# Mixed adapter values in the idle rows of the third down tile, and the next body's gate products ahead of the end of this one

## Chip, cores and metric

One NeuronCore of one Trainium2 chip runs the whole kernel. The metric is the device time of one launch, in microseconds (us), as the median of three runs. In what follows PE is the matrix engine (TensorE), DVE is VectorE, ACT is ScalarE, POOL is GpSimd and SP is SyncE, which only issues transfers here.

## What is computed

A gated state-space layer is followed by a mixture of experts; both are added to `x` (4 batches of 512 tokens, width 512). The change lies in the mixture's down projections. Cut to that, with E = 64 mask slots in 8 groups (experts) of 8 adapters of rank 8, I = 352 hidden values:

```
def _fused_linear(x, W, qa, qb, scale, w):
    out = x @ W.T
    a = einsum('th,krh->tkr', x, qa)
    b = einsum('tkr,khr->tkh', a, qb)
    mix = einsum('tkh,tk->th', b, w)
    return out + scale[None, :] * mix
def expert(...):
    xe = x + w @ muW.T
    gate = silu(_fused_linear(xe, gW, gqa, gqb, gs, w))
    up = _fused_linear(xe, uW, uqa, uqb, us, w)
    return _fused_linear(gate * up, dW, dqa, dqb, ds, w)
```

For the down projection of one expert, `x` above is `gate * up` (512 tokens by 352 values), `a` times `w` are 8 x 8 = 64 mixed adapter values for each token, and `qb` takes those 64 to the 512 outputs. A sum over the 8 experts, weighted per token, and the two halves of a shared expert are added to the layer's input.

## The kernel before

Every float is split into a high part (rounded to the type that PE takes here) and a low part (the rest), and a product is three matmuls: high by high, high by low, low by high. All matmuls have 512 columns at most. There are four batches (b = 0 to 3); each has ten bodies, `s = 10 b` to `10 b + 9`: two for the halves of the shared expert and eight for the experts, e = 0 to 7 (**routed** bodies). Beside the routed bodies of batch b, ACT, DVE and POOL work through the state-space scan of batch b + 1 (64 tiles, ten in most bodies), so batch 3 has none. The 64 tiles of batch 0 come ahead of the first body, and in batch 0 the weights of bodies 3 to 9 are also split on the way (ACT `hi`, DVE and POOL `lo_piece`) and stored to scratch memory; later batches load them from there. The engines' order is written out by hand, one function per engine and body, and semaphores tie them together.

What PE does in a routed body (`routed` in the tensor block):

- `up(s, m, 0)` and `up(s, m, 1)` for the three tiles of hidden values (128, 128 and 96 of them): 12 matmuls each, gate products into bank `bg[m]` (b_g0, b_g1, b_g0), up products into `bu[m]` (b_u0, b_u1, b_u0), and 8 half-height adapter matmuls after each pair. `up_waits(s, 0)` waits for the weights `gm0`, for DVE to be done with the third hidden tile of the body before, and for `dve_dawf` of the body before, since that was read from b_g0. `up(s, 0, 1)` waits for the first add of the body before, which frees b_u0.
- `qa`, `qa_mask`: 13 matmuls for the next body's adapters, into b_q.
- `down(s, tc, ms)`: for one of four groups of 128 tokens (tc) and some of the three hidden tiles (ms) three matmuls per tile: 9 in all for one bank. The third hidden tile fills 96 of the 128 rows. The banks by tc are b_g1, b_u1, b_q, b_u0.
- `adapter_a`: nine matmuls into b_g0, after which `pe_a` tells DVE.
- `adapter_b(s, tc)`: two matmuls into the same bank as `down(s, tc)`: `daw_s` by the high and by the low part of `qb`. `pe_dn` is raised after the second. The four groups go in the order 3, 0, 1, 2 (`DONE`).

Between `adapter_a` and `adapter_b` three steps run on other engines: `daw_first` (DVE: mixed adapter values `dawf` from b_g0), `daw_round` (ACT: high part `rnd`), `daw_low` (DVE: `daw_s`, whose rows 0 to 63 hold the high part and rows 64 to 127 the low part; `dawf` holds its 64 values twice). `add_down` (DVE) then adds each finished bank to `xx`, in the order of `DONE`. In bodies with scan tiles DVE has further work between these: a tile's scan between `daw_first` and `daw_low` (slot e), the low part of `qb` and another tile after `daw_low` (slot f), then the adds, then two tiles (slot a) and the first `hidden` of the next body, which waits for ACT's tanh and with it for `pe_gu`, raised by PE after `up(s, 0, 1)` and its adapters.

In e = 7 the scan is over; in batches 0 to 2 PE there transposes the next batch's normalised input in two steps (`xn_transposed`), one before and one after `down(s, 2)`.

SP issues all weight transfers in program order. In the bodies of batch 0 from 3 on `raw_store` writes each finished tile to scratch (`dwt`, down weights, in one transfer, `dqt`, the adapters' down weights `qa` and `qb`, in one); the store of a tile stands ahead of the next load into the raw buffer that it came from.

Of the kernel before, what the change touches and what calls it, by code (L numbers as in the profile page):

```python
# [26 lines left out]
P = 128  # L27
# [10 lines left out]
IC = 3  # L38
# [18 lines left out]
def gated_ssm_moe(nc, x, ctxT, gu, dd, pre, rr, cst, inv, out):  # L57
    with ExitStack() as ctx:
# [13 lines left out]
        Q_D = IC * P + H  # L72
# [176 lines left out]

        pe_lgT, act_lgT, pe_lg, dve_rt, act_ex, pe_wdT, act_wdT, pe_fl = (  # L250
# [48 lines left out]
        def scaled(kind, s):  # L299
            return 2 * (s - 3) + (1 if kind == "qb" else 2)  # L300

# [45 lines left out]
        def _(sp):  # L347
# [47 lines left out]
            def store(kind, s):  # L395
                sp.dma_start(scr[kind][w_index(s)], tile_of[kind][:].bitcast(F32).rearrange("p a n -> p (a n)")
                             ).then_inc(dma_st[kind], 16)
# [9 lines left out]
            def load(kind, s):  # L407
                free(sp, kind, s)
                sp.wait_ge(dma_st[kind], 16 * stored_before(kind, s))
                sp.dma_start(tile_of[kind][:].bitcast(F32).rearrange("p a n -> p (a n)"), scr[kind][w_index(s)]  # L410
                             ).then_inc(dma_t[kind], 16)
# [179 lines left out]
        def _(pe):  # L591
# [212 lines left out]
            def down(s, tc, ms=range(IC)):  # L804
# [14 lines left out]
                for m in ms:  # L819
                    if tc == 0:  # L820
                        pe.wait_ge(dve_hl, IC * s + m + 1)
                    n = 3 * m
                    k = slice(0, IW[m])
                    o = m * H
                    for v, hl_ in ((hh, 0), (hl, 0), (hh, 1)):
                        i = mm(down_bank(s, tc)[:], v[k, m, t], dwt[k, hl_, o:o + H], start=(n == 0),  # L826
                               stop=(n == 8 and not is_routed(s)))
                        n += 1
                return i

# [131 lines left out]
        def _(act):  # L962
# [6 lines left out]
            def hi(kind, s):  # L969
                k = piece[kind, s]  # L970
                act.wait_ge(dma_raw[slot_of[k]], 16 * use_of[k])
                if kind in ("dq", "qb"):
                    act.wait_ge(pool_scale, scaled(kind, s))
                free(act, kind, s)
                need(act, dma_st[kind], 16 * stored_before(kind, s))
                rounded(tile_of[kind][:, 0], raw[slot_of[k]][:, 0:width[kind]]).then_inc(act_hi[slot_of[k]], 1)

            def hi_0(n):
# [4 lines left out]
                if n >= 4 and (kind[0] == "g" or kind == "dw"):  # L983
                    act.wait_ge(dma_st[kind], 16 if s == 2 else 32)
# [36 lines left out]
            def round_ctx(nb):  # L1021
                act.wait_ge(dma_ctx, 16 * (nb + 1))
                if nb > 0:
                    need(act, pe_dn, LC * NX * (nb - 1))
                    for k in ("dq", "qb"):
                        act.wait_ge(dma_st[k], 16 if nb == 1 else 16 * NF)
# [435 lines left out]
        def _(dve):  # L1462
# [481 lines left out]
```

## Time and profile before

| what | value |
|---|---|
| runs | 1695.51 us (median of 3), 1692.44 to 1696.01 |
| profiled execution: span from first to last instruction | 1685.8 us |
| PE busy | 1568.4 us (93%), 6856 matmuls |
| DVE busy | 1155.5 us (69%) |
| POOL busy | 737.8 us (44%) |
| ACT busy | 617.2 us (37%) |
| chain of work that ended last | PE 63%, DVE 18%, issue 5%, ACT 5%, POOL 4%, DMA 3% |

The profile comes from one execution, whose span is the second row. Its time from outside isn't listed; the median of the runs is 9.7 us above the span, which is what lies before the first and after the last instruction, together with the difference between executions. PE's busy time counts each matmul from its start to a modelled end, and neighbours overlap; how close matmuls follow each other is read from the starts in the timeline.

### The profile page before, as it was taken

The page shows a single profiled execution, that of the slowest core. Times are in us where ns is not written, and L with a number is a line of the kernel's source. Part 1 is how long each engine was busy: PE and PEld are TensorE (multiplying, and loading weights), DVE is VectorE, ACT ScalarE, POOL GpSimd, SP SyncE. Part 2 cuts the span into 40 slices and gives each one's busy share as a digit, 9 for nine tenths or more (in the row PEclk, how much of TensorE's full clock was granted, in tenths as well). Part 3 has the DMA queues.
Part 4 walks back from the last instruction along what each step waited for, and adds up shares of the span by engine and source line. Part 5 has one row for each costly group of instructions (what it writes and reads, how often), then busy time and mean ns, then how long its engine had stood idle before and what let it go on. Part 6 is the DMA issues. An engine that isn't in the chain of part 4 may idle for free.

```text
span 1685.8 us, 19547 instructions
## 1 busy us (share of the span) xinstructions
PE 1568.4 (93%) x6856; PEld 1155.1 (69%) x6856; DVE 1155.5 (69%) x1634; ACT 617.2 (37%) x971; POOL 737.8 (44%) x537
## 2 busy tenths in 40 slices
PE   3787799798888999999999999999999999999999
PEld 2343377566666677777777777777777777777776
DVE  5798964788999867487888755778888553333333
ACT  5545443444454434443343244333433321111111
POOL 4488510489898801077777301376786000000000
PEclk8799999899999999999999999999999999999999
DMA  7688627688787664765667445587665456566552
GB/s 251 215 285 315 254 80 253 201 290 297 270 289 286 253 255 172 248 228 205 232 238 258 152 161 196 202 275 257 238 208 180 175 200 210 184 222 222 195 181 85
DMA packets 111473, 375.87 MB, mean 223 GB/s; under 512 B 20176, under 2 KB 45776, under 8 KB 94864
## 3 DMA queue, kind: packets, MB, share of 16 engines
q1 hardware_dynamic: 101904, 340.81, 57.8%
q10 hardware_dynamic: 9472, 33.82, 5.8%
q8 instruction: 55, 0.90, 0.2%
q14 instruction: 42, 0.34, 0.1%
HBM read 304.33 MB, written 70.25 MB: 222 GB/s over the span
## 4 chain that ended last, share of the span: by engine, by line
PE 63%; DVE 18%; issue 5%; ACT 5%; POOL 4%; DMA 3%; SPq 0%; ACTq 0%; DVEq 0%; POOLq 0%
PE b_g L735 14%; PE b_u L735 14%; PE b_u L826 7%; DVE ring L1493 4%; PE b_g L826 3%; PE b_q L781 3%; PE b_q L826 3%; PE b_g L799 2%; DVE ring L1499 2%; PE b_g L766 2%; DVE tt L1467 2%; POOL ring L1392 2%; PE b_g L759 1%; POOL yx L1401 1%; DVE z L1467 1%
## 5 line engine op out<-in xcount | busy, mean ns | idle before, releaser
L1392 POOL TENSOR_TENSOR ring<-du,rep 128x512 f32<-128x512 f32 x256 | 344.5, 1349 | 151.4 <-DVE du L1571 91.9
L735 PE MATMUL b_g<-xnb,gm 128*128 128x512 f32 (+1 forms) x1440 | 356.2, 396 | 0.9 <-DVE xnb L1470 0.9
L735 PE MATMUL b_u<-xnb,gm 128*128 128x512 f32 (+1 forms) x1440 | 349.1, 391 | 0.0
L1493 DVE TENSOR_TENSOR_SCAN ring<-b_a,ring 128x512 f32<-128x512 f32 x256 | 310.8, 1214 | 15.7 <-ACT b_a L964 8.4
L1401 POOL TENSOR_TENSOR yx<-yx,ring 128x512 f32<-128x512 f32 x192 | 261.8, 1364 | 130.4 <-DVE ring L1499 129.9
L735 PEld LDWEIGHTS b_g<-xnb,gm 128*128 128x128 f32 (+1 forms) x1440 | 252.1, 179 | 89.1 <-issue 24.6
L735 PEld LDWEIGHTS b_u<-xnb,gm 128*128 128x128 f32 (+1 forms) x1440 | 257.1, 179 | 71.1
L1467 DVE SCALAR_TENSOR_TENSOR tt<-tt,b_g 128x512 f32<-128x512 f32 (+1 forms) x120 | 82.1, 684 | 222.7 <-ACT tt L964 222.5
L964 ACT ACTIVATE b_a<-delta,a_neg 128x512 f32<-128x512 f32 x256 | 173.6, 681 | 113.9 <-DVE ring L1493 113.9
L964 ACT ACTIVATE tt<-b_g 128x512 f32<-128x512 f32 (+1 forms) x120 | 71.1, 593 | 316.7 <-PE b_u L766 286.3
L826 PE MATMUL b_u<-dwt,hhl 128*128 128x512 f32 (+1 forms) x720 | 185.4, 394 | 0.0
L826 PEld LDWEIGHTS b_u<-dwt,hhl 128*128 128x128 f32 (+1 forms) x720 | 135.7, 189 | 30.0 <-issue 0.5
L1470 DVE TENSOR_TENSOR hhl<-tt,hhl 128x512 fp32r<-128x512 f32 (+1 forms) x120 | 89.9, 749 | 84.4 <-ACT hhl L964 84.4
L964 ACT ACTIVATE hhl<-tt 128x512 fp32r<-128x512 f32 (+1 forms) x120 | 75.4, 628 | 177.8 <-DVE tt L1467 177.8
L1499 DVE TENSOR_TENSOR ring<-ring,b_d 128x512 f32<-128x512 f32 x192 | 126.7, 660 | 0.0
L826 PE MATMUL b_g<-dwt,hhl 128*128 128x512 f32 (+1 forms) x360 | 100.1, 401 | 12.7 <-issue 7.4
L781 PE MATMUL b_q<-xnb,qat 128*128 128x512 f32 x384 | 97.7, 404 | 4.7 <-DVE qat L1470 4.7
L799 PE MATMUL b_g<-hhl,dqt 128*128 128x512 f32 (+1 forms) x288 | 77.5, 409 | 25.5 <-DVE tt L1467 13.6
L781 PEld LDWEIGHTS b_q<-xnb,qat 128*128 128x128 f32 x384 | 71.0, 191 | 30.0 <-issue 8.9
L826 PEld LDWEIGHTS b_g<-dwt,hhl 128*128 128x128 f32 (+1 forms) x360 | 67.1, 191 | 32.7 <-issue 10.0
L1467 DVE SCALAR_TENSOR_TENSOR tt<-tt,b_u 128x512 f32<-128x512 f32 (+1 forms) x120 | 82.2, 685 | 4.1
L799 PEld LDWEIGHTS b_g<-hhl,dqt 128*128 128x128 f32 (+1 forms) x288 | 53.8, 194 | 45.0 <-issue 17.6
(254 smaller groups left out, 2120.2 us busy)
## 6 DMA issues: line engine op xcount, KB each, us to landing
gm<-scr_gm SPq DMA_DIRECT2D x64, 1024.0 KB, 6.8
dwt<-scr_dw SPq DMA_DIRECT2D x32, 1536.0 KB, 6.8
rep<-bc_d ACTq DMA_DIRECT2D x64, 512.0 KB, 5.8
gm<-scr_gm SPq DMA_DIRECT2D x32, 768.0 KB, 4.4
dqt<-scr_dq SPq DMA_DIRECT2D x25, 896.0 KB, 9.1
scr_gm<-gm SPq DMA_DIRECT2D x20, 1024.0 KB, 7.5
scr_dw<-dwt SPq DMA_DIRECT2D x10, 1536.0 KB, 6.2
qat<-scr_qa SPq DMA_DIRECT2D x25, 512.0 KB, 10.2
```

The source lines that it names most:

```text
L735: i = mm(out_b[0:IW[m], :], w, v, start=(n == 0), stop=(n == 11 and not is_routed(s)))
L766: i = mm(out_b[0:IW[m], :], qbt[rows, hl_, cols], v[rows, :], start=False, stop=(k == 2))
L781: mm(b_q[:], w, v, start=(n == 0), stop=False)
L799: i = mm(b_g0[:], w, v, start=(n == 0), stop=(n == 8))
L826: i = mm(down_bank(s, tc)[:], v[k, m, t], dwt[k, hl_, o:o + H], start=(n == 0), stop=(n == 8 and not is_routed(s)))
L964: return nc.scalar.activation(out_, in_, func, **k)
L1392: v.tensor_tensor(ring[:, T % NRING], du[:, T % 4, :], rep[:, N % NREP, 0], ALU.mult).then_inc(pool_dbu, 1)
L1401: v.tensor_tensor(yd, yd, ring[:, T % NRING], ALU.add).then_inc(pool_y, 1)
L1467: return v.scalar_tensor_tensor(out=out_, in0=a, scalar=s_, in1=b_, op0=op0, op1=op1)
L1470: return tt_(out_, whole, hi_.bitcast(F32), ALU.subtract)
L1493: v.tensor_tensor_scan(w, ba[T % 2][:], w, 0.0, ALU.mult, ALU.add).then_inc(dve_scan, 1)
L1499: tt_(w, w, c_bank(nb)[:], ALU.mult).then_inc(dve_p, 1)
```

## The change

The 64 mixed adapter values times high and low part of `qb` need 192 operand rows (high by high, high by low, low by high). Two matmuls with 128 rows held them. Now 128 of them are one operand, and the other 64 use the 32 idle rows of the third hidden tile, in two of its three matmuls:

- `daw_s` rows 0 to 31 and again 32 to 63: high part of values 0 to 31; rows 64 to 127: low part of all 64. The matching `dqt` rows hold the high part of `qb` 0 to 31, the low part of the same, and the high part of all. `adapter_b` is one matmul.
- `hh[96:128, 2]`: high part of values 32 to 63; `dwt[96:128]` of the third tile holds the high and the low part of `qb` for them. So the two matmuls of `down(s, tc, (2,))` with `hh` have 128 rows; the one with `hl` keeps 96.
- PE's order: after `adapter_a` come the first two hidden tiles of groups 2 and 3, then the first gate products of the next body (`up(s + 1, 0, 0)`; not in e = 7), then a wait for `daw_s` and its roundings, then for each group the third tile and `adapter_b`.
- ACT: `daw_round` has three instructions (128, 32 and 32 rows) where it had one. DVE: `daw_low` works on 64 rows where it had 128.
- In batch 0 two more transfers inside the on-chip memory put `qb` where it is wanted (`dma_pl`; PE waits for both in bodies 3 to 9), the store of `dwt` is two transfers and that of `dqt` five. Loads of `dqt` from scratch leave out what isn't read: 1280 of 1792 columns.

```diff
+        QA = IC * P
+        Q_D = QA + H
+        Q_ALL = Q_D + QA
+        W2 = slice(2 * H, 3 * H)
+        C0, C0B, C0C, C1 = (slice(k * 32, (k + 1) * 32) for k in range(4))
...
             def store(kind, s):
+                to_w = scr["dw"][w_index(s)].rearrange("p (a n) -> p a n", a=2)
+                if kind == "dw":
+                    rows = HID if is_routed(s) else slice(0, P)
+                    sp.dma_start(to_w[:, :, 0:2 * H], dwt[:, :, 0:2 * H].bitcast(F32)).then_inc(dma_st[kind], 16)
+                    sp.dma_start(to_w[rows, :, W2], dwt[rows, :, W2].bitcast(F32)).then_inc(dma_st[kind], 16)
+                    return
+                if kind == "dq":
...
+                    sp.dma_start(to_w[C1, :, W2], q[C1]).then_inc(dma_st[kind], 16)
+                    if s > 2:
+                        sp.dma_start(q[C0B, 0], q[C0, 1]).then_inc(dma_pl, 16)
+                        sp.dma_start(dwt[C1, :, W2].bitcast(F32), q[C1]).then_inc(dma_pl, 16)
+                    return
...
             def down(s, tc, ms=range(IC)):
...
                 for m in ms:
-                    if tc == 0:
+                    full = m == IC - 1 and is_routed(s)
+                    if tc == 0 and not full:
                         pe.wait_ge(dve_hl, IC * s + m + 1)
                     n = 3 * m
-                    k = slice(0, IW[m])
                     o = m * H
                     for v, hl_ in ((hh, 0), (hl, 0), (hh, 1)):
+                        k = slice(0, P if full and v is hh else IW[m])
...
             def adapter_b(s, tc):
                 t = slice(tc * P, (tc + 1) * P)
-                if tc == DONE[0]:
-                    pe.wait_ge(dve_daw, rho(s) + 1)
-                q = slice(IC * P, IC * P + H)
-                mm(down_bank(s, tc)[:], daw_s[:, t], dqt[:, 0, q], start=False, stop=False)
-                mm(down_bank(s, tc)[:], daw_s[:, t], dqt[:, 1, q], start=False, stop=True
-                   ).then_inc(pe_dn, 1)
+                mm(down_bank(s, tc)[:], daw_s[:, t], dqt[:, 0, QA:Q_D], start=False, stop=True).then_inc(pe_dn, 1)
...
             def routed(b, e, post):
                 s = NX * b + 2 + e
-                up_waits(s, 0)
-                up(s, 0, 0)
+                if e == 0:
+                    up_waits(s, 0)
+                if e == 0:
+                    up(s, 0, 0)
                 up(s, 0, 1)
...
-                down(s, 0, (2,))
-                down(s, 1, (2,))
-                down(s, 2)
+                down(s, 2, (0, 1))
+                down(s, 3, (0, 1))
                 if post:
                     xn_transposed(b + 1, (2, 3))
-                down(s, 3)
+                if e < NF - 1:
+                    up_waits(s + 1, 0)
+                    up(s + 1, 0, 0)
+                if 2 < s < NX:
+                    pe.wait_ge(dma_pl, 32 * (s - 2))
+                pe.wait_ge(dve_daw, rho(s) + 1)
+                pe.wait_ge(act_daw, 3 * (rho(s) + 1))
                 for tc in DONE:
+                    down(s, tc, (2,))
                     adapter_b(s, tc)
...
             def daw_round(s):
                 act.wait_ge(dve_dawf, rho(s) + 1)
-                rounded(rnd[:], dawf[:]).then_inc(act_daw, 1)
+                rounded(daw_s[:], dawf[:]).then_inc(act_daw, 1)
+                rounded(hh[C1, 2], dawf[C1]).then_inc(act_daw, 1)
+                act.wait_ge(act_daw, 3 * rho(s) + 1)
+                rounded(daw_s[C0B], dawf[C0]).then_inc(act_daw, 1)
...
             def daw_low(s):
-                dve.wait_ge(act_daw, rho(s) + 1)
-                stt(daw_s[:], rnd[:].bitcast(F32), mlo[:], dawf[:], ALU.mult, ALU.add).then_inc(dve_daw, 1)
+                dve.wait_ge(act_daw, 3 * rho(s) + 1)
+                lo(daw_s[HALF:P], dawf[HALF:P], daw_s[HALF:P]).then_inc(dve_daw, 1)
```

On PE, the end of a routed body and the start of the next stood so before, from `adapter_a` (into b_g0) on; `x9` is nine matmuls in a row, gm0 are the next body's weights:

```order
L799 MATMUL b_g0<-hhl,dqt 128x512 x9
L826 MATMUL b_g1<-dwt,hhl 128x512 x3
L826 MATMUL b_u1<-dwt,hhl 128x512 x3
L826 MATMUL b_q<-dwt,hhl 128x512 x9
L826 MATMUL b_u0<-dwt,hhl 128x512 x9
L836 MATMUL b_u0<-dqt,daw_s 128x512
L837 MATMUL b_u0<-dqt,daw_s 128x512
L836 MATMUL b_g1<-dqt,daw_s 128x512
L837 MATMUL b_g1<-dqt,daw_s 128x512
```

The same place of the changed kernel, whose line numbers are its own:

```order
L832 MATMUL b_g0<-hhl,dqt 128x512 x9
L860 MATMUL b_q<-dwt,hhl 128x512 x6
L860 MATMUL b_u0<-dwt,hhl 128x512 x6
L768 MATMUL b_g0<-xnb,gm0 128x512 x12
L860 MATMUL b_u0<-dwt,hhl 128x512 x3
L867 MATMUL b_u0<-dqt,daw_s 128x512
L860 MATMUL b_g1<-dwt,hhl 128x512 x3
L867 MATMUL b_g1<-dqt,daw_s 128x512
L860 MATMUL b_u1<-dwt,hhl 128x512 x3
L867 MATMUL b_u1<-dqt,daw_s 128x512
L860 MATMUL b_q<-dwt,hhl 128x512 x3
L867 MATMUL b_q<-dqt,daw_s 128x512
```

24 matmuls lie between `adapter_a` and the first use of `daw_s` in both, 12 of them now from the next body; after that come 8 matmuls before and 16 now, and the next body's up products follow directly.

On ACT, around the rounding of the mixed values in a body with scan tiles, in the changed kernel (`b_a` is a scan tile's exponentials, `qbt` the high part of the next body's split `qb`); before, the first of the three wrote `rnd` and the other two weren't there:

```order
L1001 ACTIVATE b_a0<-delta,a_neg 128x512
L1001 ACTIVATE daw_s<-dawf 128x512
L1001 ACTIVATE hhl<-dawf 32x512
L1001 ACTIVATE daw_s<-dawf 32x512
L1001 ACTIVATE b_a1<-delta,a_neg 128x512
L1001 ACTIVATE b_d<-rep 128x512
L1001 ACTIVATE qbt<-raw3 128x352
```

The exponentials, the copy to b_d and `qbt` stand two instructions further back.

## Rows read from the trace of the kernel before

**Rows 1.** The page: PE's busy time, and PE's busy tenths in 40 slices.

```profile
PE 1568.4 (93%) x6856; PEld 1155.1 (69%) x6856; DVE 1155.5 (69%) x1634; ACT 617.2 (37%) x971; POOL 737.8 (44%) x537
...
PE   3787799798888999999999999999999999999999
```

**Rows 2.** Windows, routed bodies of batches 0 to 3: length, busy times, clock, DMA share.

```profile
331.57:583.57 252.00, 224.39 (x973) 164.48 (x972) 230.87 (x268) 116.19 (x176) 222.98 (x153) 0.97 0.80 281
728.93:981.04 252.11, 249.84 (x1154) 189.61 (x1153) 203.04 (x288) 94.67 (x152) 165.01 (x123) 1.00 0.63 223
1088.68:1340.82 252.14, 249.87 (x1155) 189.62 (x1154) 203.04 (x288) 94.67 (x152) 165.03 (x123) 1.00 0.63 221
1434.39:1679.92 245.53, 245.53 (x1123) 186.49 (x1121) 80.25 (x117) 34.03 (x55) 0.00 (x0) 1.00 0.53 183
```

**Rows 3.** Timeline of PE, end of a body of batch 3: start, duration, line, operation.

```profile
1606.38 0.85 PE L826 MATMUL b_g<-dwt,hhl 96*128 96x512 f32 x3
...
1607.75 2.24 PE L826 MATMUL b_q<-dwt,hhl 128*128 128x512 f32 x9
...
1611.89 0.39 PE L836 MATMUL b_u<-dqt,daw_s 128*128 128x512 f32 x1
...
1613.48 0.39 PE L837 MATMUL b_q<-dqt,daw_s 128*128 128x512 f32 x1
```

**Rows 4.** Timeline of DVE and ACT, the same stretch; in brackets idle time and releaser.

```profile
1606.58 0.69 DVE L1705 TENSOR_TENSOR dawf<-b_g,wr 128x512 f32<-128x512 f32 x1 [2.51 <-PE b_g L799]
...
1607.30 0.63 ACT L964 ACTIVATE rnd<-dawf 128x512 fp32r<-128x512 f32 x1 [3.96 <-DVE dawf L1705]
...
1607.97 0.75 DVE L1467 SCALAR_TENSOR_TENSOR daw_s<-rnd,mlo,dawf 128x512 fp32r<-128x512 f32 x1 [0.70 <-ACT rnd L964]
```

**Rows 5.** Timeline, three engines, end of a body of batch 0 (e = 4).

```profile
493.74 0.83 ACT L964 ACTIVATE gm<-raw 128x768 fp32r<-128x768 f32 x1
...
494.80 2.24 PE L826 MATMUL b_q<-dwt,hhl 128*128 128x512 f32 x9
...
496.27 0.63 ACT L964 ACTIVATE rnd<-dawf 128x512 fp32r<-128x512 f32 x1 [1.12 <-DVE dawf L1705]
...
497.43 0.48 ACT L964 ACTIVATE qbt<-raw 128x352 fp32r<-128x352 f32 x1
...
497.87 1.61 DVE L1467 SCALAR_TENSOR_TENSOR daw_s<-rnd,mlo,dawf 128x512 fp32r<-128x512 f32 x1
...
499.40 1.41 DVE L1470 TENSOR_TENSOR qbt<-raw,qbt 128x352 fp32r<-128x352 f32 x1
...
499.54 0.50 PE L836 MATMUL b_u<-dqt,daw_s 128*128 128x512 f32 x1 [0.43 <-DVE daw_s L1467]
```

**Rows 6.** Timeline of ACT: two instructions of 512 columns, one behind the other.

```profile
470.34 0.62 ACT L964 ACTIVATE hhl<-tt 128x512 fp32r<-128x512 f32 x1
470.86 0.62 ACT L964 ACTIVATE qat<-raw 128x512 fp32r<-128x512 f32 x1
```

**Rows 7.** Timeline of DVE, batch 1: last add of one body, first hidden of the next.

```profile
767.09 0.74 DVE L1467 SCALAR_TENSOR_TENSOR xx<-b_q,scal,xx 128x512 f32<-128x512 f32 x1
...
773.67 0.69 DVE L1467 SCALAR_TENSOR_TENSOR tt<-tt,b_g 128x512 f32<-128x512 f32 x1 [2.41 <-ACT tt L964]
```

**Rows 8.** Timeline of SP, store of `dqt`; DMA issues: size, us to landing.

```profile
477.35 0.33 SPq L396 DMA_DIRECT2D scr_dq<-dqt  x1
...
scr_dq<-dqt SPq DMA_DIRECT2D x8, 896.0 KB, 7.9
```

**Rows 9.** Timeline of PE in batch 0, and the window around it (clock: third last).

```profile
403.44 2.90 PE L799 MATMUL b_g<-hhl,dqt 128*128 128x512 f32 x6 [2.22 <-DVE tt L1467]
...
403.40:406.00 2.60, 2.56 (x6) 1.82 (x6) 1.60 (x2) 0.90 (x2) 2.52 (x3) 0.50 1.04 430
```

**Rows 10.** Timeline, end of the program: PE's last matmul and DVE's last add.

```profile
1681.51 0.39 PE L837 MATMUL b_q<-dqt,daw_s 128*128 128x512 f32 x1
...
1682.56 0.74 DVE L1467 SCALAR_TENSOR_TENSOR xx<-b_q,scal,xx 128x512 f32<-128x512 f32 x1
```

More of the change, by code:

```diff
@@ L71, in gated_ssm_moe @@
         PW = [2 * HC * IW[m] for m in range(IC)]
-        Q_D = IC * P + H
+        QA = IC * P
[3 more added lines that the diff above has]
+        C0, C0B, C0C, C1 = (slice(k * 32, (k + 1) * 32) for k in range(4))
+        HID = slice(0, IW[2])
         gm = [sb("gm%d" % m, [P, 2, PW[m]], F32R) for m in range(IC)]
@@ L248, in gated_ssm_moe @@
             sem(n) for n in ("pe_yt", "dve_x1", "act_nx", "pe_xnT", "act_xnh", "dve_xnl"))
+        dma_pl = sem("dma_pl")
         pe_lgT, act_lgT, pe_lg, dve_rt, act_ex, pe_wdT, act_wdT, pe_fl = (
@@ L300, in scaled, with stored @@
             return 2 * (s - 3) + (1 if kind == "qb" else 2)
+        def stored(kind):
+            return {"dw": 32, "dq": 80}.get(kind, 16)
         def stored_before(kind, s):
@@ L395, in store @@
             def store(kind, s):
+                to_w = scr["dw"][w_index(s)].rearrange("p (a n) -> p a n", a=2)
[5 more added lines that the diff above has]
+                if kind == "dq":
+                    to = scr[kind][w_index(s)].rearrange("p (a n) -> p a n", a=2)
+                    q = dqt[:, :, QA:Q_D].bitcast(F32)
+                    sp.dma_start(to[:, :, 0:QA], dqt[:, :, 0:QA].bitcast(F32)).then_inc(dma_st[kind], 16)
+                    sp.dma_start(to[C0, 0, QA:Q_D], q[C0, 0]).then_inc(dma_st[kind], 16)
+                    sp.dma_start(to[C0B, 0, QA:Q_D], q[C0, 1]).then_inc(dma_st[kind], 16)
+                    sp.dma_start(to[HALF:P, 0, QA:Q_D], q[HALF:P, 0]).then_inc(dma_st[kind], 16)
+                    sp.dma_start(to_w[C1, :, W2], q[C1]).then_inc(dma_st[kind], 16)
[3 more added lines that the diff above has]
+                    return
                 sp.dma_start(scr[kind][w_index(s)], tile_of[kind][:].bitcast(F32).rearrange("p a n -> p (a n)")
@@ L408, in load @@
                 free(sp, kind, s)
-                sp.wait_ge(dma_st[kind], 16 * stored_before(kind, s))
+                sp.wait_ge(dma_st[kind], stored(kind) * stored_before(kind, s))
+                if kind == "dw" and is_routed(s):
+                    sp.wait_ge(dma_st["dq"], stored("dq") * (1 if s == 2 else NF))
+                if kind == "dq":
+                    sp.dma_start(dqt[:].bitcast(F32).rearrange("p a n -> p (a n)")[:, 0:Q_ALL],
+                                 scr[kind][w_index(s)][:, 0:Q_ALL]).then_inc(dma_t[kind], 16)
+                    return
                 sp.dma_start(tile_of[kind][:].bitcast(F32).rearrange("p a n -> p (a n)"), scr[kind][w_index(s)]
@@ L974, in hi @@
                 free(act, kind, s)
-                need(act, dma_st[kind], 16 * stored_before(kind, s))
+                need(act, dma_st[kind], stored(kind) * stored_before(kind, s))
                 rounded(tile_of[kind][:, 0], raw[slot_of[k]][:, 0:width[kind]]).then_inc(act_hi[slot_of[k]], 1)
@@ L983, in hi_0 @@
                 if n >= 4 and (kind[0] == "g" or kind == "dw"):
-                    act.wait_ge(dma_st[kind], 16 if s == 2 else 32)
+                    act.wait_ge(dma_st[kind], stored(kind) * (1 if s == 2 else 2))
                 rounded(tile_of[kind][:, 0], src[:, 0:width[kind]]).then_inc(act_s0, 1)
@@ L1025, in round_ctx @@
                     for k in ("dq", "qb"):
-                        act.wait_ge(dma_st[k], 16 if nb == 1 else 16 * NF)
+                        act.wait_ge(dma_st[k], stored(k) * (1 if nb == 1 else NF))
                 for c in range(DM // P):
```

## The prediction

> **What bounds the kernel now.** I read the page first: PE is busy for 93% of the span, and from the tenth slice or so its digits are almost all 9 [rows 1]. Busy time alone says little, since neighbouring matmuls overlap in it, so next I read windows over the routed bodies of each batch [rows 2]. In batches 1 and 2 PE is busy for 249.8 of 252.1 us, in batch 3 for all of 245.5 us, at full clock; each window holds seven bodies, so one takes 36.0 and 35.1 us. Batch 0 is another case: its window holds only six bodies, 42.0 us each, with DVE busy for 230.9 and POOL for 223.0 of 252 us; PE waits for them. So a matmul less is worth its place in PE's stream in batches 1 to 3, and next to nothing in most of batch 0. The third view is PE's timeline at the end of a body in batch 3 [rows 3]. The place of one matmul is the distance of starts, not the 0.39 us that each row shows as its duration: seven places from 1611.89 to 1613.48 make 0.227 us each, six with 96 rows from 1606.38 to 1607.75 make 0.228, 18 with 128 rows and with 96 by turns from 1607.75 to 1611.89 make 0.230.
>
> **What the change removes.** `adapter_b` issues one matmul where it issued two, for 4 token groups in 32 routed bodies: 128 fewer, 4 per body, 4 x 0.227 = 0.91 us of PE per body and 29.1 us in all. The third hidden tile's matmuls get 128 rows instead of 96; the places just read (0.228 and 0.230) say that rows cost nothing. Nothing replaces the removed matmuls on PE.
>
> **What it moves on PE.** Between `adapter_a` and the first use of `daw_s` lie 24 matmuls now as before, 5.5 us (1606.38 to 1611.89). The cover stays, but has a new wait inside it: after 12 matmuls, 2.7 us, `up_waits` wants `dawf`, which was read from b_g0. In batch 3 `dawf` is done by 1607.30, when ACT starts on it, 0.9 us after `adapter_a` [rows 3, 4]: no wait. In the busiest bodies of batch 0 it is late: adapter_a's successors began six matmuls ahead of 494.80, at 493.4, and ACT could start at 496.27 [rows 5], 2.8 us later, so PE waits some 0.1 us there. The weights gm0 are wanted 12 matmuls and one adapter stage earlier in the stream; their load is issued when this body's first up products end, some 7 us into it (29 places), and they are wanted at some 29 us; a transfer of about that size lands in 7.9 us [rows 8]. Nothing is charged.
>
> In e = 7 there is no next gate product and only 12 matmuls remain as cover. In batch 3 the wait comes at 1606.38 + 2.73 = 1609.11 on these rows' scale; the third rounding ends at 1608.96 (next part): just in time. In batches 0 to 2 sixteen transposes stand there too. Nothing is charged.
>
> **What it adds on ACT and DVE.** ACT rounds three times. Instructions of 512 columns follow each other every 0.52 us, and one takes 0.62 us [rows 6]; I take the same for 32 rows. The third ends 0.52 + 0.52 + 0.62 = 1.66 us after the first begins. `daw_s`, which DVE finishes after the first, ended 1.42 us after it in batch 3 (1607.30 to 1608.72) [rows 4] and 3.2 us after it in the loaded body (496.27 to 499.48) [rows 5]. So ACT is 0.24 us later than DVE at most, and the cover has 2.9 us to spare in batch 3. `daw_low` is kept at its present price though it has half the rows; if it fell to half of 0.75 us nothing on PE's path would move.
>
> What stands behind the roundings on ACT comes 1.04 us later: a tile's exponentials, and in batch 0 the high part of `qb`, for which DVE's low part waits. In the body of rows 5 it would end at 497.91 + 1.04 = 498.95, before DVE gets there at 499.40: hidden. Other bodies of batch 0 have less room, since `daw_s` takes 1.61 us there and 0.75 us elsewhere [rows 4, 5]. Bounds: 0, and 7 x 1.04 = 7.3 us. I take 1.5 us, nearer to the row that hides it. In batches 1 and 2 no `qb` is split, and the exponentials are needed by the tile after `daw_s`, 2.3 us or more after the first rounding begins.
>
> **The adds.** `pe_dn` now rises every four matmuls (0.91 us) instead of every two (0.45), so the last add ends later. Before, it started 1.05 us after the last matmul's start [rows 10], because four adds of 0.74 us queue up: 7 x 0.227 + 1.05 = 2.64 us after the first adapter matmul. Now it can start some 0.45 us after the last matmul's start, 15 x 0.227 + 0.45 = 3.86 us after that point. That is 1.2 us later, and the next body's first `hidden` is released 0.91 us earlier. DVE waited 2.41 us for it in batch 1 [rows 7]; 0.3 us is left. Bodies that have less are behind with their adds anyway, and the new spacing doesn't show there. I charge 1.0 us for the two batches; the other end is the second rival. At the end of the program the last add starts 0.6 us earlier.
>
> **Transfers.** From body 3 on in batch 0 SP issues nine transfers where it issued two, 0.33 us each or more [rows 8], so the load behind them, of the next body's third gate tile, goes out 2.3 us later. At 477 us it would land by about 488, and ACT rounds that tile at 493.74 [rows 5]: hidden. The bounds are 0 and 7 x 2.3 = 16 us, if ACT waited in full everywhere; I take 0, by that row. PE's new wait for the two moves is far off: the `dqt` store of rows 8 is issued at 477.35, such a store lands in 7.9 us, and PE wants the result at 499.54, 22 us later. Bytes hardly change, and DMA engines are 63% busy in batches 1 and 2 [rows 2]. Nothing is charged. Ahead of the first body SP issues seven more; nothing to 2.3 us, taken as 0 for the same reason.
>
> **The clock.** In batch 0 the place saved becomes idle time of PE. After 2.22 us of idle time PE ran at a granted clock of 0.50, its lower level of 1.2 GHz, and six matmuls took 2.90 us [rows 9], against 5 x 0.227 + 0.39 = 1.5 at 2.4 GHz. The Trainium skill (TensorE: Matmul & The Clock Gate, Part 1) states that an idle PE falls back to half rate until it has been busy again; the trace agrees here. By the rows as they stand I add nothing, since PE isn't the bound in those bodies; by the rule more of them would fall, which is the third rival.
>
> **The sum.** Batch 3: 8 x 0.91 = 7.3 and 0.6 at the end. Batches 1 and 2: 16 x 0.91 - 1.0 = 13.6. Batch 0: 0.9 for e = 7, nothing for the other seven, less 1.5 for ACT. In all 20.9 us, so the span goes from 1685.8 to 1664.9 us. The median of the runs is 9.7 us above that execution's span; with the same distance the forecast is **1674.5 us**, 1.2% faster. A measurement of this kernel can tell about 0.2%, 3.4 us.
>
> **The rivals.**
>
> 1. *Batch 0 pays too.* If DVE's chain there starts from PE more often than it seems, seven more bodies give 0.91 us and ACT's 1.5 us doesn't show: 28.8 us, 1666.7 us. Against it: DVE is busy for 92% of batch 0's window. Chance 0.10.
> 2. *DVE takes over in batches 1 and 2.* DVE has 0.3 us left at the start of a body by my count. If it has none, it sets the pace in the seven scan bodies of each batch and 14 x 0.91 - 1.0 = 11.7 us more are lost: 9.2 us gained, 1686.3 us; half of it 1680.4. Against it: DVE is busy for only 203 of 252 us and catches up inside the body. Chance 0.15, mostly in part.
> 3. *The clock in batch 0.* Six bodies fall to the lower level once more. On rows 9's scale that is 1.4 us for six matmuls, and 8 us if all six show in full: 1682.9 us. Against it: full clock for the rest of each body gives PE room. Chance 0.05.
> 4. *Slower: b_u0 isn't free.* The next up products now come 16 matmuls (3.6 us) after the wait instead of 20, and need DVE's first add, which stands behind a scan tile. It turns into a loss when PE waits over 29.7 / 21 = 1.4 us in each of the 21 scan bodies; with 2 us each, 42 - 29.7 = 12 us are lost: 1708 us. For it: in batch 0 DVE is already late (PE waited 0.43 us for `daw_s` [rows 5]). Against it: in batch 1 the last of four adds starts 6.6 us before DVE's next work for PE, and the first one, three adds before, sooner still. Chance 0.04.
>
> That PE's stream isn't shorter at all is ruled out by its order, which has four matmuls less in each routed body and the others in full.
>
> **How the numbers follow.** The forecast has a chance of 0.66; its own range is 1671 to 1679, from a few us of stores and ACT's rounding either way. Taking in half of the first, second and third rivals gives **1668 to 1683 us** for 8 in 10. Faster by over 0.2%: all but the fourth rival and the worst of the second and third, 0.94; within 0.2%: 0.02; slower: 0.04.
>
> **What would show it.** PE has 128 matmuls fewer. Routed bodies take 35.1 us instead of 36.0 in batches 1 and 2 and 34.2 instead of 35.1 in batch 3; in batch 0 about 42 us as now. DVE's wait before the first `hidden` in batch 1 shrinks from 2.41 to about 0.3 us. Waits of PE for the moves don't appear. I am wrong if bodies of batch 3 don't shrink by 0.9 us (then matmuls weren't the price), if those of batches 1 and 2 shrink by less than 0.6 us with DVE as releaser (second rival), or if batch 0 changes by more than 4 us either way.

## Result and profile after

The changed kernel takes **1675.5 us** (median, 1674.2 to 1679.0), beside 1694.0 us for the kernel before on the same chip (1689.3 to 1696.0): ratio 0.9911, 95% interval [0.9893, 0.9930]. The quotient of the two medians is 0.9891; in what follows the ratios and intervals of the record are used. In two later comparisons the ratio was 0.9905 [0.9884, 0.9926] and 0.9886 [0.9864, 0.9908]. (In the last of them one execution of the changed kernel, the profiled one, took 8539 us; it is left out of the median, and its trace isn't read.) So the change makes the kernel faster by 0.9 to 1.1%; the forecast of 1674.5 us and its range hold. The sum behind it doesn't hold in all its terms, as the profile shows. The profiled execution has a span of 1672.3 us, 13.5 us below the 1685.8 us of the kernel before, where 20.9 were forecast.

The page of the changed kernel (busy times; PE in 40 slices; the chain of waits by engine):

```profile
PE 1550.7 (93%) x6728; PEld 1134.1 (68%) x6728; DVE 1161.0 (69%) x1634; ACT 657.3 (39%) x1035; POOL 737.0 (44%) x537
...
PE   3777889888888899999999999999999999999999
...
PE 61%; DVE 18%; ACT 6%; issue 5%; DMA 5%; POOL 4%; SPq 1%; ACTq 0%; DVEq 0%; POOLq 0%
```

PE has 128 matmuls less and 17.7 us less busy time than in [rows 1]; it still bounds the routed bodies of batches 1 to 3. New is the DMA share of the chain, 5% where it was 3%. Since the change moves matmuls across the end of a body, bodies are best counted from the start of the last `adapter_a` matmul to the next one. Windows between that place in the first and in the last routed body of batches 1, 2 and 3 (columns as in [rows 2]; seven bodies each), for the kernel before:

```profile
723.17:972.56 249.39, 247.84 (x1138) 188.03 (x1137) 204.86 (x288) 94.37 (x152) 166.48 (x124) 1.00 0.64 225
1082.92:1332.34 249.42, 247.86 (x1139) 188.04 (x1137) 204.86 (x288) 94.37 (x152) 166.50 (x124) 1.00 0.63 223
1428.65:1674.18 245.53, 245.53 (x1123) 186.49 (x1122) 80.25 (x117) 34.03 (x55) 0.00 (x0) 1.00 0.53 183
```

and for the changed kernel:

```profile
727.20:972.66 245.46, 242.16 (x1110) 182.73 (x1109) 207.32 (x288) 102.93 (x166) 166.87 (x124) 1.00 0.64 221
1082.13:1327.02 244.89, 242.13 (x1110) 182.74 (x1109) 207.31 (x288) 102.93 (x166) 166.86 (x124) 1.00 0.63 220
1422.44:1661.85 239.41, 239.41 (x1094) 181.35 (x1093) 81.74 (x117) 42.83 (x69) 0.00 (x0) 1.00 0.53 180
```

Batch 3 gains 6.1 us in its seven bodies, 0.87 each, and PE has no idle time there. Batches 1 and 2 gain 3.9 and 4.5, and PE's idle time in them rose from 1.6 to 3.3 and 2.8 us. PE's timeline at the end of a body of batch 3, the place of [rows 3]:

```profile
1593.74 2.22 PE L832 MATMUL b_g<-hhl,dqt 128*128 128x512 f32 x9
1595.80 1.53 PE L860 MATMUL b_q<-dwt,hhl 128*128 128x512 f32 x6
...
1598.53 2.88 PE L768 MATMUL b_g<-xnb,gm 128*128 128x512 f32 x12
1601.24 0.86 PE L860 MATMUL b_u<-dwt,hhl 128*128 128x512 f32 x3
1601.94 0.40 PE L867 MATMUL b_u<-dqt,daw_s 128*128 128x512 f32 x1
...
1604.74 0.40 PE L867 MATMUL b_q<-dqt,daw_s 128*128 128x512 f32 x1
1604.97 1.30 PE L768 MATMUL b_u<-xnb,gm 128*128 128x512 f32 x5
```

No row has a wait in brackets: from 1595.80 to 1604.97 stand 40 matmuls, four fewer than before. The body is 34.65 us long, from one last `adapter_a` matmul to the next, where it was 35.53 us. The roundings on ACT in the same body, the place of [rows 4]:

```profile
1596.72 0.63 ACT L1001 ACTIVATE daw_s<-dawf 128x512 fp32r<-128x512 f32 x1 [3.96 <-DVE dawf L1745]
1597.38 0.63 ACT L1001 ACTIVATE hhl<-dawf 32x512 fp32r<-32x512 f32 x1
1598.03 0.63 ACT L1001 ACTIVATE daw_s<-dawf 32x512 fp32r<-32x512 f32 x1
```

The starts are 0.65 us apart, not the 0.52 us of [rows 6], so the third ends 1.94 us after the first begins; PE wants it 2.6 us later. And DVE in batch 1, the place of [rows 7]:

```profile
773.28 0.75 DVE L1507 SCALAR_TENSOR_TENSOR xx<-b_q,scal,xx 128x512 f32<-128x512 f32 x1 [0.18 <-PE b_q L867]
...
777.76 0.69 DVE L1507 SCALAR_TENSOR_TENSOR tt<-tt,b_g 128x512 f32<-128x512 f32 x1 [0.31 <-ACT tt L1001]
```

The last add no longer follows the one before it at once: it waits 0.18 us for PE. It starts 9.6 us after the last `adapter_a` matmul of its body, where it was 8.4, and DVE's idle time before the next body's first `hidden` fell from 2.41 to 0.31 us, as forecast.

**Where the bodies lose.** PE's waits in batches 1 and 2 (us in all, times, longest) are those of the kernel before, row by row, and one more:

```profile
PE b_g L832 <- DVE hhl L1510: 3.1, 4, 1.3
PE b_q L814 <- DMA qat<-scr_qa: 2.9, 2, 1.7
PE b_g L832 <- DVE tt L1507: 1.6, 1, 1.6
```

It falls on two bodies that gain nothing: the second routed body (e = 1) of batch 1 takes 36.47 us instead of 35.54, that of batch 2 35.89 instead of 35.54, while their neighbours take 34.59 instead of 35.46. PE's timeline there, and SP's (first the load of `dwt`, then that of `qat`):

```profile
753.90 0.39 PE L799 MATMUL b_u<-awp,qbt 64*96 64x512 f32 x1
...
756.03 1.19 PE L814 MATMUL b_q<-xnb,qat 128*128 128x512 f32 x4 [1.74 <-DMA qat<-scr_qa]
```

```profile
736.82 0.32 SPq L443 DMA_DIRECT2D dwt<-scr_dw  x1
...
741.78 0.43 SPq L443 DMA_DIRECT2D qat<-scr_qa  x1
```

The load of `qat` is issued 5 us behind that of `dwt`, since `dqt`, `xx`, `ws`, `wr` and `gqt` stand between, and lands 14.2 us after its issue (the longest in the view of `qat`), at 756.0. The kernel before, same body:

```profile
730.93 0.32 SPq L410 DMA_DIRECT2D dwt<-scr_dw  x1
...
735.93 0.38 SPq L410 DMA_DIRECT2D qat<-scr_qa  x1
```

```profile
751.05 1.20 PE L781 MATMUL b_q<-xnb,qat 128*128 128x512 f32 x4
```

There it took 13.6 us and landed at 749.5, 1.5 us ahead of its use. SP is held at the load of `dwt`, which the end of the body before releases. From there to the use of `qat` there were 20.1 us; now, at 754.2 without the wait, there would be 17.4. The difference of 2.7 us is the twelve gate matmuls that were moved ahead of the body's end.

A smaller loss stands in no row of PE's waits. In the bodies e = 4 and 5 of batches 1 and 2 DVE comes late to `dawf`, which ends 2.9 us after the start of the last `adapter_a` matmul; in all other bodies of batches 1 to 3 it ends after 1.1 to 2.3 us. The moved gate products overwrite the bank that it is read from, so they need it done after some 12 places, 2.7 us. DVE, and PE's weight load for the first of them, in batch 1:

```profile
835.64 0.68 DVE L1745 TENSOR_TENSOR dawf<-b_g,wr 128x512 f32<-128x512 f32 x1
...
836.44 1.69 PEld L768 LDWEIGHTS b_g<-xnb,gm 128*128 128x128 f32 x8 [0.29 <-issue]
```

The weight load starts 0.12 us behind the end of `dawf`; the profile names no releaser, but the last of the program's waits there is the one for `dawf`. These four bodies gain 0.69 to 0.72 us in place of 0.87, and are the only ones in which this place in PE's stream comes late.

### The profile page after: what moved, and what is told of

It reads as the page before. It is cut to its first block, busy times and chain, and to the rows that moved or that the text cites. A ratio compares the mean times of both kernels' runs of the same rounds, so it can differ in the third digit from the quotient of the medians.

```text
span 1672.3 us, 19443 instructions
## 1 busy us (share of the span) xinstructions
PE 1550.7 (93%) x6728; PEld 1134.1 (68%) x6728; DVE 1161.0 (69%) x1634; ACT 657.3 (39%) x1035; POOL 737.0 (44%) x537
## 4 chain that ended last, share of the span: by engine, by line
PE 61%; DVE 18%; ACT 6%; issue 5%; DMA 5%; POOL 4%; SPq 1%; ACTq 0%; DVEq 0%; POOLq 0%
PE b_g L768 14%; PE b_u L768 13%; PE b_u L860 8%; DVE ring L1533 4%; PE b_g L860 3%; PE b_q L814 3%; PE b_q L860 3%; PE b_g L832 3%; DVE ring L1539 2%; PE b_g L799 2%; DVE tt L1507 2%; DMA qat<-scr_qa 2%; POOL ring L1432 2%; PE b_g L792 1%; PE b_d L753 1%
## 5 line engine op out<-in xcount | busy, mean ns | idle before, releaser
L1533 DVE TENSOR_TENSOR_SCAN ring<-b_a,ring 128x512 f32<-128x512 f32 x256 | 310.9, 1215 | 20.9 <-POOL ring L1432 10.4
L860 PE MATMUL b_u<-dwt,hhl 128*128 128x512 f32 (+1 forms) x720 | 190.8, 394 | 0.8 <-issue 0.7
```

The costliest lines, as they stand in the source:

```text
L1533: v.tensor_tensor_scan(w, ba[T % 2][:], w, 0.0, ALU.mult, ALU.add).then_inc(dve_scan, 1)
```

## Experiments

Beside the times, one measure is read from every trace: the start of the last `adapter_a` matmul in the first routed body (A), from there to the same place of batch 1's first routed body (B: batch 0), and on to the last routed body (C: batches 1 to 3). In us:

| kernel | A | B | C | span |
|---|---|---|---|---|
| before | 325.8 | 397.4 | 951.0 | 1685.8 |
| changed | 330.2 | 397.0 | 934.7 | 1672.3 |
| changed, again | 323.6 | 400.0 | 934.9 | 1668.9 |
| changed, qat first | 326.0 | 399.2 | 931.7 | 1667.3 |
| the same, again | 326.2 | 399.2 | 931.7 | 1667.5 |
| merge only | 328.1 | 403.7 | 960.6 | 1702.9 |
| move only | 330.1 | 400.3 | 954.6 | 1696.8 |
| move only, qat first | 329.3 | 401.8 | 950.9 | 1693.7 |
| changed, second matmul | 330.7 | 403.1 | 954.5 | 1699.7 |
| before, stores cut up | 323.2 | 398.8 | 951.0 | 1684.7 |
| before, ACT two more | 326.3 | 401.1 | 951.0 | 1690.0 |
| changed, qat first, 4 more | 327.1 | 400.5 | 931.7 | 1669.7 |
| changed, qat first, 16 more | 327.2 | 419.1 | 931.7 | 1688.3 |

C repeats to 0.2 us; A scatters by 6.6 us between two traces of the same program, and B by 3. The first matmul that the change moves or removes stands behind A. So effects are read from C where they can be.

**1. The wait for qat.** The theory: loads queued behind the body's end came 2.7 us nearer to their use. The rival: DVE's adds hold those two bodies.

```diff
             for s in range(NB):
...
+                qa_early = 1 < i < NX - 1 and from_scratch(s + 1)
+                if qa_early:
+                    next_pieces(s + 1, ("qa",))
                 if s > 0:
                     next_pieces(s, ("dw",))
```

with "qa" taken out of the later call.

> The changed kernel with one thing moved: in the bodies whose weights come from scratch, SP issues the load of the next body's qat before the load of dwt. My theory: in the changed kernel PE waited 1.7 us at 754.3 us and 1.2 us in the same body of batch 2 for qat, because the gate products that were moved up bring everything behind them 12 places (2.7 us) nearer to the end of the body before, which is what releases dwt and all loads that SP has queued behind it. With qat ahead of dwt that wait is gone: 2.9 us less, 1672.6 us, and bodies 9 and 17 take some 35 us like their neighbours. Rival (DVE's adds, not the load, hold these two bodies): no change, 1675.5 us, and PE's wait there names DVE instead.

Measured: 1669.9 us, 0.9886 [0.9869, 0.9902]; C is 2.9 us shorter, bodies e = 1 take 34.70 and 34.67 us, and no wait of PE names the transfer. In the view of `qat` the time from issue to landing (least, median, most) went from the first row to the second:

```profile
DMA to landing us min/median/max: 4.3/9.4/14.2
```

```profile
DMA to landing us min/median/max: 3.1/4.6/8.8
```

The theory holds, in size too.

**2. The two halves of the change, each alone.** Merge only: the changed kernel with `up_waits(s, 0)` and `up(s, 0, 0)` back at the start of every routed body.

```diff
-                if e < NF - 1:
-                    up_waits(s + 1, 0)
-                    up(s + 1, 0, 0)
                 if 2 < s < NX:
                     pe.wait_ge(dma_pl, 32 * (s - 2))
```

> The changed kernel with the next body's first gate products back where they were, behind the end of the body. What is left as cover between adapter_a and the first use of daw_s is 12 matmuls, 2.7 us, in place of 24. Matmuls as in the changed kernel. My theory: in batches 1 to 3 the third rounding ends 0.9 + 1.66 = 2.6 us after adapter_a, so nothing or 0.1 to 0.3 us per body is lost, and the wait for qat (2.9 us) goes; in batch 0 the roundings end some 4.5 us after adapter_a, so PE stands up to 1.8 us in some seven bodies, partly in idle time that it has anyway. Together 1673 to 1684 us. Rival (the move is what pays for most of the gain): 1685 us or more, with PE's waits for ACT or DVE in front of the third tile in every body.

Measured: 1704.4 us, 1.0080 [1.0067, 1.0093]: a miss, and the rival's number. PE waits 34.5 us for `daw_s`, in 21 bodies (PE's waits: us in all, times, longest):

```profile
PE b_u L860 <- DVE daw_s L1505: 34.5, 21, 3.2
```

In batch 3 the body of 35.53 us becomes 34.95 to 35.03: the merge works there, less 0.36 us, since the third rounding ends 1.94 us after the first begins. In batches 1 and 2 my estimate had left out what DVE does between. Its timeline in the body e = 4 of batch 1, and PE's wait:

```profile
882.75 0.68 DVE L1740 TENSOR_TENSOR dawf<-b_g,wr 128x512 f32<-128x512 f32 x1
883.35 1.21 DVE L1528 TENSOR_TENSOR_SCAN ring<-b_a,ring 128x512 f32<-128x512 f32 x1
884.48 0.66 DVE L1534 TENSOR_TENSOR ring<-ring,b_d 128x512 f32<-128x512 f32 x1
885.17 0.69 DVE L1505 TENSOR_TENSOR daw_s<-dawf,daw_s 64x512 fp32r<-64x512 f32 x1
```

```profile
885.92 0.96 PE L860 MATMUL b_u<-dwt,hhl 128*128 128x512 f32 x3 [2.23 <-DVE daw_s L1505]
```

A scan tile stands on DVE between `dawf` and `daw_s`, in the kernel before too; 24 matmuls hide it and 12 don't. After such waits PE's clock falls as well, which it does in batches 1 and 2 of no other kernel here (window; the clock is third last):

```profile
884.00:892.00 8.00, 6.08 (x20) 4.84 (x21) 6.30 (x9) 3.23 (x6) 6.59 (x5) 0.79 0.21 66
```

Move only: the kernel before with the next gate products ahead of the first `adapter_b` (and at the start of a body for e = 0 alone).

```diff
                 down(s, 3)
+                if e < NF - 1:
+                    up_waits(s + 1, 0)
+                    up(s + 1, 0, 0)
                 for tc in DONE:
                     adapter_b(s, tc)
```

> The kernel before with only the move: the next body's first gate products stand ahead of the first adapter_b, and adapter_b keeps its two matmuls of daw_s. My theory: the price is the number of matmuls, and that is as before; the cover grows from 24 to 36 matmuls, which nothing needed, and the loads behind the end of the body come 12 places nearer to their use, so the wait for qat costs 2.9 us: 1694.0 + 2.9 = 1697 us. Rival (the order itself brings part of the gain, by filling PE's waits): 1690 us or less.

Measured: 1704.4 us, 1.0087 [1.0073, 1.0100]. C grew by 3.6 us, and the waits for `qat` are 3.5:

```profile
PE b_q L781 <- DMA qat<-scr_qa: 3.5, 2, 2.1
```

That is as expected. Of the rest of the 13 us the trace shows 7.3 ahead of batch 1, which I had not expected: 3.0 in B, and 4.3 in A, which ends before the first moved matmul and can't come from the move. The move with qat first tells this part from the waits for `qat`:

> The kernel before with the move of the next body's first gate products, and with the load of qat ahead of that of dwt. The move alone took 13 us more than the kernel before, of which its trace showed 3.6 us as waits for qat. My theory: the waits go and the rest was clock and batch 0, 3 to 9 us either way; 1694 to 1700 us against some 1691, with bodies of batches 1 to 3 as long as in the kernel before. Rival (the move has a price of its own in PE's order): bodies in batches 1 and 2 stay longer than before, and the time stays at 1704 us.

Measured: 1699.2 us, 1.0050 [1.0032, 1.0067]; C is that of the kernel before to 0.1 us. So in batches 1 to 3 the move neither gains nor costs once `qat` is early. A + B are 7.9 us longer than before in this trace too, 3.5 of them in A; the end of the next section says what is open there.

**3. The price of a place.** Each matmul of `daw_s` twice, with the rest of the change in place.

```diff
+                mm(down_bank(s, tc)[:], daw_s[:, t], dqt[:, 0, QA:Q_D], start=False, stop=False)
                 mm(down_bank(s, tc)[:], daw_s[:, t], dqt[:, 0, QA:Q_D], start=False, stop=True).then_inc(pe_dn, 1)
```

> The changed kernel with each matmul of daw_s issued twice, so that PE has the 128 matmuls again (the sum then holds that product twice). My theory: PE's places are the price, 4 x 0.227 = 0.91 us in each of the 24 bodies of batches 1 to 3 and in one of batch 0: 1675.5 + 22.7 = 1698 us, a little above the kernel before by what the wait for qat takes. Rival (most of the gain came from elsewhere, from order or the stored form): 1690 us or less.

Measured: 1699.3 us, 1.0051 [1.0037, 1.0065]; C is 19.9 us longer than in the changed kernel, 0.86 us in each of 23 bodies. Bodies without a wait are 35.49 us long (35.46 before, 34.59 changed): the four places are the whole of such a body's gain; the rest of the change, the shorter load of `dqt` among it, gives such a body nothing of its own.

**4. Stores and ACT.** In the kernel before, the two stores cut into as many pieces as SP issues in the changed kernel:

```diff
+                    for c in (slice(0, 2 * H), slice(2 * H, 3 * H)):
+                        sp.dma_start(to[:, :, c], dwt[:, :, c].bitcast(F32)).then_inc(dma_st[kind], 16)
```

and for `dqt` likewise, by rows and columns.

> The kernel before with its stores of dwt and dqt cut into as many pieces as SP issues in the changed kernel: two for dwt in place of one, and for dqt seven in batch 0 and five for the first routed body in place of one. My theory: the loads behind them are issued some 2.3 us later per body and still land in time, 0 to 2 us in all: the time is within 0.2% of the kernel before. Rival (SP's queue holds up the rounding of the next tiles): up to 7 x 2.3 = 16 us more, with ACT waiting for raw in batch 0.

Measured: 1692.4 us, 1.0011 [0.9996, 1.0025]; B 398.8 and C 951.0, and A the earliest of all. The pieces cost at most 4 us by the interval, and nothing that the trace shows. ACT's two further roundings, in the kernel before:

```diff
                 rounded(rnd[:], dawf[:]).then_inc(act_daw, 1)
+                act.wait_ge(act_daw, rho(s) + 1)
+                rounded(hh[96:P, 2], rnd[96:P])
+                rounded(hl[96:P, 2], rnd[96:P])
```

> The kernel before with two more instructions on ACT behind the rounding of dawf, each of 32 rows and 512 columns (they round rnd into rows that nothing reads). My theory: ACT's next work comes 1.04 us later; in batch 0 that shows in some bodies only, 0 to 2 us in all, so the time is within 0.2% of the kernel before. Rival (DVE's low part of qbt waits in each of seven bodies): 7.3 us more, 0.4%.

Measured: 1690.9 us, 0.9994 [0.9977, 1.0011]. The bound of 7.3 us is excluded; what ACT does behind the roundings is hidden.

**5. What is lost ahead of the first body.** The changed kernel once more, unedited:

> The changed kernel once more, unedited, on the chip of the next runs. My theory: the 4.4 us by which its first routed body was late in the trace shown come from one stretch at the lower granted clock, at 169 to 176 us, and not from the change (the move alone, which stores as the kernel before, had the same stretch and the same 4.3 us, and the changed kernel with qat ahead of dwt, which has all the new stores, had neither). So here the last adapter_a matmul of the first routed body starts between 325.5 and 331 us, late by some 4 us only if a stretch at the lower clock stands near 170 us, and the time is 0.989 to 0.992 of the kernel before. Rival (the new stores make it late): 330 us whatever the clock does.

Measured: 1674.0 us, 0.9905 [0.9884, 0.9926], A = 323.6 us. The same stretch of the scan, between the starts of the same two matmuls, in the first trace and in this one (windows; the clock is third last):

```profile
169.48:175.80 6.32, 6.32 (x10) 3.15 (x11) 5.17 (x6) 3.33 (x6) 2.15 (x3) 0.52 0.90 352
```

```profile
167.22:170.52 3.30, 3.30 (x10) 1.81 (x10) 3.30 (x4) 1.64 (x4) 2.09 (x3) 1.00 1.00 416
```

One program has this stretch at a clock of 0.52 (nearly all of it at the lower of the two levels, 1.2 GHz) and at 1.00, which is 3.0 of the 6.6 us between the two traces; over all of A the mean clock is 0.89 and 0.92. So the 4.4 us of the first trace are scatter of executions, not the change. What places the stretches at the lower level in time was not found.

**6. Work put back into batch 0.** To see whether the saved places raise PE's idle time and lower the clock, the kernel with qat first got four and then sixteen matmuls more per routed body of batch 0, by issuing the first matmul of groups 2 and 3 anew:

```diff
+                        if n == 0 and tc > 1 and 1 < s < NX:
+                            for _ in range(8):
+                                mm(down_bank(s, tc)[:], v[k, m, t], dwt[k, hl_, o:o + H], start=True, stop=True)
```

(2 in place of 8 for the four). Beside them ran the changed kernel and the one with qat first, both unedited.

> The changed kernel, unedited, for a direct comparison with the three kernels below on the same chip. Expected at 0.990 to 0.992 of the kernel before, with some 0.971 as the mean granted clock of its runs where the kernel before has 0.974.

> The changed kernel with the load of qat ahead of that of dwt, unedited since its first run. My theory: two waits of 1.5 to 1.8 us go, so it is 3 us below the changed kernel, 0.9985 of it; ratio to the kernel before 0.988 to 0.990. Rival (the first result was a lucky clock): level with the changed kernel.

> The changed kernel with qat first, and in the routed bodies of batch 0 four more matmuls per body: the first matmul of the third and of the fourth token group is issued three times over the same bank, each time starting anew, so the sum is as it was. PE has in batch 0 what the change took from it. Theory of the clock: less idle time of PE in batch 0 leaves fewer stretches at the lower granted clock, so the mean clock of the runs rises from 0.971 or 0.972 to 0.974 and the time falls by up to 3 us in spite of the work. Rival (the stretches at the lower clock are scatter that the change doesn't cause, and batch 0 is bound by DVE): no change within 2 us, as the work lies in PE's idle time.

> As the kernel with four more matmuls per body of batch 0, with sixteen (the two first matmuls are issued nine times each), 3.6 us of PE per body. Theory of the clock: PE's idle time in batch 0, some 6 us per body, is more than halved, and the mean clock reaches 0.975 or more; the time is that of the kernel without them or up to 4 us less. Rival (scatter): the clock stays at 0.972, and the time grows by 0 to 10 us, since in bodies where PE comes close to being the bound the sixteen show.

Measured: changed 1671.4 us, 0.9886 [0.9864, 0.9908]; qat first 1668.9 us, 0.9868 [0.9848, 0.9888]; four more 1671.1 us, 0.9888 [0.9864, 0.9912]; sixteen more 1690.9 us, 0.9998 [0.9982, 1.0015]. The mean granted clocks of the runs are 0.972, 0.974, 0.973 and 0.974, and 0.973 for the kernel before: filling PE's idle time did not raise the clock of the runs, so the theory of the clock is not borne out. (Over B alone the traces have 0.97 and 0.96 with qat first, 0.98 with four and 0.98 with sixteen more; with one or two executions each that tells nothing.) My bound for the sixteen was missed by a factor of two: B grew by 19.9 us, of 8 x 16 x 0.2175 = 27.8 that they would cost in a body bound by PE. So in batch 0 some 70% of added PE work in this place shows, although without it DVE is busy for 90% of the first six bodies (238.4 of 263.9 us).

**The better version.** Qat first is 2.5 us below the changed kernel by the medians of the one direct comparison, and 4.2 us by its first ratio, set against the 0.9911 of the earlier comparison (0.0025 of 1691 us). The intervals of the ratios overlap, so the times alone don't prove it; C, shorter by 2.9 to 3.2 us in each pair of traces, does for the part that it covers.

## Why the prediction was right, and which of its terms were not

- **Count of matmuls.** Right, and the main term. A place that goes is worth 0.87 / 4 = 0.2175 us, where I took 0.227 from starts inside the row. Over 23 bodies that is 0.9 us less than in the sum.
- **Cover on PE.** Right for the changed kernel: no wait for `daw_s` in batches 1 to 3 except in e = 7. My figure for three roundings was too small (1.66, measured 1.94). In the last body, where I saw "just in time", the first matmul of `daw_s` comes 4.01 us after the last of `adapter_a`; 16 places would be 3.6, so PE waits 0.4 us there. And the cover was worth more than the prediction said: without the moved products the merge loses more than it gains. The new wait inside the cover, for `dawf`, was charged nothing, by a body of batch 3 and 0.1 us in batch 0; in four bodies of batches 1 and 2 it costs 0.15 to 0.2 us each, 0.7 us in all.
- **The adds.** Mechanism right: the last add starts 1.2 us later, and 0.31 us of DVE's idle time are left. Of the 1.0 us charged nothing shows, since PE's waits for DVE in batches 1 and 2 have the sizes that they had before. That the charge was nearly made up for by the wait for `dawf`, which was left out, is luck.
- **Transfers: the step that failed.** "Nothing is charged" looked at loads that are issued later and at `gm0`, whose use is earlier. But the move brings the use of everything behind the moved products, `qat` first, nearer to the release of `dwt`, at which SP's queue stands. It cost 2.9 us in the first trace and 3.2 in the second.
- **Stores, moves between tiles, ACT.** Right: PE never waits for the moves, and 0 is inside both intervals; the 1.5 us for ACT need not have been charged.
- **Batch 0.** Forecast a loss of 0.6 us in the eight bodies; B is 397.0 to 400.0 us in four traces of the changed kernel with and without qat first, and 397.4 to 401.1 in three traces with the old order on PE. No gain, as forecast, but perhaps for another reason: sixteen more matmuls do show there, and kernels with the move and the old number of matmuls have 400.3 to 403.1. That suggests that the merge gains 2 to 4 us in batch 0 and the move loses as much; with a scatter of 3 us it isn't settled.
- **The sum.** C has 23 bodies, for which the terms give 23 x 0.91 - 1.0 = 19.9 us. Measured: 16.4 in the changed kernel and 19.3 with qat first. So of the 3.5 us missing 2.9 are `qat`; the other 0.6 are the smaller place (0.9) and the wait for `dawf` (0.7), less the 1.0 charged for the adds. The tail, from the last `adapter_a` matmul to the end, gave 1.2 us where the terms give 1.5 (0.91 for the last body's places, 0.6 for the last add), as PE waits 0.4 us for `daw_s` there. In the trace shown A took back 4.4 us: 16.4 + 0.4 (B) + 1.2 - 4.4 = 13.6, the difference of the spans. In the second trace A gave 2.2 us more instead.
- **The distance from span to time.** The text takes 9.7 us as lying around the span. For the changed kernel's profiled execution it is 1674.17 - 1672.3 = 1.9 us. Most of the 9.7 was the difference between executions: the profiled one of the kernel before stood at the fast end (25 later runs of it go from 1685.2 to 1698.7 us). The forecast took the gain off the median of the runs, so it came out unharmed. That it came within 1.0 us is in part luck: the gain between the medians was 18.5 us, not 20.9, but the kernel before was itself 1.5 us faster than in the runs that the forecast started from (1694.0 beside 1695.5). As a ratio the forecast is 0.9876, and the first two intervals don't contain it.
- **Rivals.** The second (DVE takes over in batches 1 and 2) and the fourth (b_u0 not free) didn't come: PE's waits for DVE in batches 1 and 2 are the same as before but for those for `dawf`, and PE waited once, 0.6 us in batch 0, for an add that frees b_u0. The third was seen in a sharper form in batches 1 and 2 of the kernel with the merge only, and isn't borne out for the change itself. The fourth's break-even of 1.4 us a body divides 29.7 us, the gain of all 32 bodies before any charge; by the sum's 20.9 us it is 1.0.

**Open:** why the move without the merge, with qat first, takes 8 us more (1.0050) while C is as before. Its trace accounts for less: 3.5 us are in A, where both kernels do the same work, and 4.4 in B, where three traces with the old order differ by 3.7. Its runs have a mean granted clock of 0.970 beside 0.974 for the kernel before; whether that is cause or company wasn't separated.

## What to carry to other kernels

When a step is moved ahead of an event that releases buffers, measure the time from that event to the first use of every load queued behind it, not only of the loads that the moved step reads. Two halves of a change can each lose alone (here 0.8 and 0.9%, of the second only the wait for `qat` explained) and gain together, when one shortens the work and the other restores the cover that the shortening took. Look for a new wait in the bodies where the engine that it waits for is latest, not in a quiet one. Use a stretch that repeats to 0.2 us as the measure where the total scatters by more than the effect.

## What the runs showed of the hardware

- One program's trace repeated to 0.2 us over 935 us of PE-bound work, while the 330 us of scan ahead of it scattered by 6.6 us: there PE idles between tiles, and its granted clock falls in one execution where it stays in another. The Trainium skill (TensorE: Matmul & The Clock Gate, Part 1) has an idle PE fall back to half rate; the trace agrees that it falls where PE idles, and shows that one program's idle time may or may not bring it about.
- The three roundings of 512 columns started 0.65 us apart, the second too, which waits for nothing; the two of [rows 6] stood 0.52 us apart. The reason wasn't tried.
- Loads of 512 KB (`qat`) landed 9.4 us after their issue in the median of 25, and 14.2 us after it in the body shown, behind eight others; with most of them issued ahead of `dwt` it was 4.6 us in the median and 8.8 at most.
- That one engine is busy for 90% of a stretch (DVE in batch 0) didn't make work on another (PE) free: about 70% of the PE time added between `adapter_a` and `adapter_b` showed, by one trace.
